# Audio tower on one core: raw loads from a queue of their own, and a new order of calls

## The reference

```python
patches = x[:, :, :n * 16].reshape(B, 90, n, 16) ... -> (B, n, 1440)
h = einsum('bnf,ef->bne', patches, W) + b                        # tokens of 192
h = h + causal_attention(layernorm(h), Wq, Wk, Wv)               # one head of 192
y = layernorm(h)
qkv = y @ W_qkv.T + b_qkv + top2_of_8_experts(y, A, B_lora)      # rank 16 each
h = h + softmax(q k^T / 4) v @ W_proj.T + b_proj                 # 12 heads of 16
```

## Time and profile before

| | |
|---|---|
| median of 3 runs | 631.27 us (631.05, 631.27, 634.49) |
| the profiled execution | 629.51 us |
| its span, first to last instruction | 627.8 us |
| PE busy | 577.8 us, 92% |
| DVE, POOL, ACT busy | 497.5, 382.3, 356.1 us (79, 61, 57%) |
| DMA engines, mean share | 61%, 83.15 MB |

### The profile page before, as it was taken

The page is one execution under the profiler, slowest core; times in us unless marked ns, Lnnn a source line. Parts: engine busy times, 40 slices in busy tenths (PEclk is TensorE's granted clock), DMA queues, the critical chain, the costliest instruction groups (busy, mean ns, idle before and its releaser), DMA issues.

```text
span 627.8 us, 20585 instructions
## 1 busy us (share of the span) xinstructions
PE 577.8 (92%) x7811; PEld 520.6 (83%) x7811; DVE 497.5 (79%) x1312; ACT 356.1 (57%) x688; POOL 382.3 (61%) x646
## 2 busy tenths in 40 slices
PE   1879879999999999999999999999999999997784
PEld 1767768888898989998999999898989898776674
DVE  6523665678888888888898989898888889998774
ACT  3637536666666575657666666666665545543431
POOL 7684887987767677677676867677676633221010
PEclk9979889999999999999999999999999999998965
DMA  8795546887675776767677768575867160615511
GB/s 196 175 209 91 132 96 149 147 193 134 166 150 134 147 169 133 171 129 162 137 164 153 165 142 173 131 155 146 157 142 135 34 127 25 131 37 95 103 28 36
DMA packets 60132, 83.15 MB, mean 132 GB/s; under 512 B 11754, under 2 KB 44087, under 8 KB 58499
## 3 DMA queue, kind: packets, MB, share of 16 engines
q1 hardware_dynamic: 60035, 81.85, 61.2%
HBM read 50.24 MB, written 13.57 MB: 102 GB/s over the span
## 4 chain that ended last, share of the span: by engine, by line
PE 79%; DMA 8%; DVE 7%; ACT 2%; issue 2%; SPq 2%; DVEq 0%; ACTq 0%
PE ps_r L1436 24%; PE ps_tok L1428 7%; PE ps_tok L1429 6%; PE ps_tok L1430 6%; PE ps_p L1688 5%; PE ps_s L1675 4%; PE ps_r L1428 4%; PE ps_r L1430 4%; PE ps_r L1429 4%; DMA k<-qk_scratch 3%; PE ps_r L1589 3%; DMA v<-L_tok_W 2%; PE ps_r L1718 2%; PE ps_r L1526 2%; DMA qk_scratch<-qk 1%
## 5 line engine op out<-in xcount | busy, mean ns | idle before, releaser
L730 POOL TENSOR_TENSOR xs<-raw,xs 90x368 f16<-90x368 f32 x188 | 162.5, 888 | 40.7 <-ACT xs L824 40.7
L1428 PE MATMUL ps_tok<-w_tok,xs 128*128 128x192 f16 x576 | 145.3, 252 | 4.0 <-DVE h L1203 1.5
L1429 PE MATMUL ps_tok<-w_tok,xs 128*128 128x192 f16 x576 | 144.3, 250 | 0.0
L1430 PE MATMUL ps_tok<-w_tok,xs 128*128 128x192 f16 x576 | 144.2, 250 | 0.0
L824 ACT ACTIVATE p2T<-ps_p 128x552 f16<-128x552 f32 x64 | 40.2, 628 | 64.0 <-PE ps_p L1688 44.0
L824 ACT ACTIVATE xs<-raw 90x736 f16<-90x736 f32 x96 | 76.4, 805 | 0.0
L1428 PEld LDWEIGHTS ps_tok<-w_tok,xs 128*128 128x128 f16 x576 | 66.2, 115 | 7.5 <-POOL xe L730 2.6
L730 POOL TENSOR_TENSOR xe<-raw,xe 90x368 f16<-90x368 f32 x64 | 55.4, 884 | 23.4 <-ACT xe L824 23.4
L1429 PEld LDWEIGHTS ps_tok<-w_tok,xs 128*128 128x128 f16 x576 | 66.8, 116 | 1.0
L1430 PEld LDWEIGHTS ps_tok<-w_tok,xs 128*128 128x128 f16 x576 | 66.2, 115 | 0.2
L957 ACT ACTIVATE qk<-ps_r,b_qk 128x368 f16<-128x368 f32 x48 | 27.2, 567 | 47.3 <-PE ps_r L1430 47.3
(11 more groups left out here) (178 smaller groups left out, 1594.8 us busy)
## 6 DMA issues: line engine op xcount, KB each, us to landing
raw<-x SPq DMA_DIRECT2D x32, 1035.0 KB, 7.7
qk_scratch<-qk SPq DMA_DIRECT2D x32, 276.0 KB, 2.8
q<-qk_scratch SPq DMA_DIRECT2D x48, 138.0 KB, 4.8
k<-qk_scratch SPq DMA_DIRECT2D x48, 138.0 KB, 5.6
xs<-xe SPq DMA_DIRECT2D x30, 184.0 KB
v<-v2s SPq DMA_DIRECT2D x64, 76.5 KB, 6.4
out<-h2b SPq DMA_DIRECT2D x16, 240.0 KB
xs<-xe SPq DMA_DIRECT2D x15, 149.5 KB
```

The costliest lines, as they stand in the source:

```text
L730: nc.gpsimd.tensor_tensor(lo, src, hi, ALU.subtract).then_inc(s_lo, 1)
L1428: mm(dst, stat[0], mov[0], start=start, stop=False)
L1429: mm(dst, stat[0], mov[1], start=False, stop=False)
L1430: return mm(dst, stat[1], mov[0], start=False, stop=stop)
```

## The change

`load_next` moves from SP's list to ACT's, so the loads of x of groups 2 to 15 are issued by ScalarE, in its own queue. It waits on the same semaphore value as before. The prologue (groups 0 and 1, token weights, early and middle weights) stays on SP as it was. `LAG`, `MOVED`, `RING_AT`, `STEPS` and the order of the calls in all five lists are new, and `MOVED` now has an entry for the first five and the last five groups instead of three. No arithmetic, tile or buffer changes; PE makes the same 758 calls.

```diff
@@ step_of
-    if op in MOVED and g < 3:
+    if op in MOVED and g < ENDS:
         return at - MOVED[op][n][g]
-    if op in MOVED and g >= GROUPS - 3:
-        return at + MOVED[op][n][g - GROUPS + 6]
+    if op in MOVED and g >= GROUPS - ENDS:
+        return at + MOVED[op][n][g - GROUPS + 2 * ENDS]
+ENDS = 5
-STEPS = 35
+STEPS = 37
@@ SP's step
-                def load_next(half):
-                    g = group(s, "load_next", half)
-                    if g is not None and g > 1:
-                        sp.wait_ge(s_lo, lows_done(g - 1, (8, 16)[half]))
-                        load_x(clips(g, half), half)
@@ ACT's step
+                def load_next(half):
+                    g = group(s, "load_next", half)
+                    if g is not None and g > 1:
+                        act.wait_ge(s_lo, lows_done(g - 1, (8, 16)[half]))
+                        nc.scalar.dma_start(raw[:, half, :, :], clips(g, half)).then_inc(s_x[half], 16)
```

More of the change, by code:

```diff
@@ L54 @@
 LOWS = [(half, blk, part) for half, blk in HIGHS for part in range(2)]
[L57 to L71, removed]
@@ L74 @@
[L74 to L91, removed]
[4 rows of a table removed]
[L96 to L107, removed]
[7 rows of a table removed]
@@ L115 @@
-STEPS = 35
-RING_AT = {"av1": 2, "pv3": 0, "qk1": 2, "cv0": 1, "qk2": 0, "xt0": 2, "cv1": 1, "ot0": 0, "ot1": 2, "pv0": 0,
-           "yt0": 1, "yt1": 0, "pr0": 2, "pr1": 1, "ga": 0, "xt1": 2, "pv1": 0, "g0": 2, "g1": 0, "v0": 1, "v1": 2,
-           "sc": 1, "at": 0, "pv2": 2, "pt": 0, "qk0": 1, "av0": 0}
+LAG = {"place_v2": (13,), "lateload": (6, 8, 9, 9, 10, 10), "extra_rows": (8,), "qk_to_scratch": (12,),
+    "stack_qk": (12,), "store": (14,), "h_to_pairs": (9,), "low": (8, 8, 8, 8, 8, 8, 8, 8, 8, 8, 8, 9, 9, 9, 9, 9),
+    "ad": (12,), "ln1": (9, 10, 10), "h2b": (13,), "ln2": (11,), "xn2": (11,), "xn2_twin": (11,),
+    "wact": (5, 5, 6, 6, 7, 9), "ga_copy": (12,), "g_high": (11, 11), "router_exp": (12,), "load_next": (7, 8),
+    "v_copy": (11, 11), "exp2": (13, 13, 13, 14), "p2t_high": (13, 13, 14, 14), "high": (8, 8, 8, 8, 8, 8, 8, 8),
+    "xn_tile": (10, 10, 10), "ad_high": (12,), "exp1": (11,), "p1t": (11,), "xn_twin": (10,), "o2_twin": (14,),
+    "cv_high": (12, 12), "qk_high": (12, 12, 12), "xn_high": (10, 10), "o_high": (14, 14), "x2_high": (11, 11),
+    "fin": (13, 13), "shift": (11, 11, 11, 12), "logits": (10,), "ranks": (10,), "g_low": (9, 9), "dispatch": (10,),
+    "wdve": (3, 5, 6, 6, 6, 7), "h_tile": (7, 7, 8), "norm2": (11, 12, 12, 12), "p2t_low": (11, 11, 12, 12),
+    "max1": (9,), "stats1": (7, 7, 8), "ad_low": (10,), "max2": (11, 11, 11, 11), "h2": (9, 9), "stats2": (9,),
+    "cv_low": (10, 10), "qk_low": (10, 10, 10), "xn_low": (8, 8), "o_low": (12, 12), "x2_low": (9, 9), "ga": (11,),
[3 rows of a table added]
@@ L123 @@
+STEPS = 37
+RING_AT = {"ga": 0, "pr1": 2, "g0": 0, "g1": 1, "v0": 2, "pv1": 0, "v1": 1, "sc": 2, "at": 0, "pv2": 1, "pt": 2,
+           "pv3": 1, "av0": 0, "av1": 2, "cv0": 1, "qk0": 0, "qk1": 2, "cv1": 1, "qk2": 0, "xt0": 2, "ot0": 1,
+           "pv0": 0, "ot1": 2, "yt0": 1, "yt1": 0, "xt1": 2, "pr0": 1}
 HIGH_AFTER = (0, 0, 0, 0, 9)
@@ L503, in unit_bank, with clips @@
             return (ps_s, ps_p)[n // 2 % 2][0:rows, n % 2, 0:cols]
+        def clips(g, half):
+            b0 = g * GB + half * (GB // 2)
+            return x_v[:, b0:b0 + GB // 2, 0:NT * PATCH]
         block = ctx.enter_context(nc.Block())
@@ L645, in store @@
                             sp.dma_start(out_v[rows, g * PAIRS:(g + 1) * PAIRS, :], h2b[rows, g % 2, :, :]).then_inc(s_out[g % 2], 16)
-                late_weights(5)
[L648 to L652, removed]
-                stack_qk()
-                late_weights(1)
-                late_weights(2)
-                late_weights(4)
-                store()
-                extra_rows()
-                load_next(0)
-                late_weights(0)
+                place_v2()
+                late_weights(1)
+                extra_rows()
+                late_weights(4)
+                qk_to_scratch()
+                late_weights(2)
+                late_weights(0)
+                stack_qk()
+                store()
+                h_to_pairs()
+                late_weights(3)
+                late_weights(5)
             for s in range(STEPS):
@@ L790, in h2b_ @@
                                                 ALU.add).then_inc(s_h2b, 1)
+                low(11)
+                low(12)
                 low(13)
                 low(14)
-                ln1(2)
                 low(15)
+                ad_()
+                ln1(1)
                 low(0)
                 low(1)
-                ln2()
-                xn2_()
-                xn2_twin()
+                ln1(2)
+                h2b_()
                 low(2)
@@ L808, in step @@
                 low(9)
+                ln2()
+                xn2_()
+                xn2_twin()
+                low(10)
                 ln1(0)
-                ln1(1)
-                ad_()
-                low(10)
-                low(11)
-                h2b_()
-                low(12)
             for s in range(STEPS):
@@ L1026, in step @@
                 weights(0)
-                p2t(2)
-                router_exp()
-                g_high(0)
-                high(5)
-                g_high(1)
-                v_copy(0)
-                high(6)
-                weights(3)
-                exp2(3)
+                weights(2)
+                ga_copy()
+                g_high(0)
+                g_high(1)
+                router_exp()
+                load_next(1)
+                v_copy(0)
+                exp2(3)
+                p2t(2)
                 v_copy(1)
-                high(7)
+                high(0)
+                weights(5)
+                xn_tile(0)
                 ad_high()
+                exp1()
                 p2t(3)
-                weights(1)
-                exp1()
-                exp2(0)
+                high(1)
+                high(2)
                 p1t()
-                xn_tile(0)
-                qk_high(0)
                 xn_tile(1)
                 xn_tile(2)
-                high(0)
-                high(1)
+                weights(1)
+                high(3)
+                xn_twin()
+                exp2(0)
+                high(4)
+                weights(3)
+                o2_twin()
+                high(5)
+                cv_high(0)
+                qk_high(0)
                 qk_high(1)
                 p2t(0)
-                cv_high(0)
-                exp2(1)
+                cv_high(1)
                 qk_high(2)
                 xn_high(0)
-                o2_twin()
-                cv_high(1)
-                weights(5)
+                exp2(1)
+                o_high(0)
+                high(6)
                 weights(4)
-                o_high(0)
-                weights(2)
                 o_high(1)
-                xn_twin()
-                high(2)
                 p2t(1)
+                load_next(0)
                 x2_high(0)
+                exp2(2)
                 x2_high(1)
-                exp2(2)
-                high(3)
-                high(4)
-                ga_copy()
                 xn_high(1)
+                high(7)
             for s in range(STEPS):
@@ L1363, in fin @@
                                                        op0=ALU.mult, op1=ALU.add).then_inc(s_fin, 1)
+                fin(0)
+                shift(3)
+                logits()
+                fin(1)
+                ranks()
+                g_low(0)
+                g_low(1)
+                dispatch()
+                weights(2)
+                h_tile(2)
+                norm2(1)
+                p2t(2)
+                weights(0)
+                max1()
+                stats1(2)
                 ad_low()
@@ L1731, in pr @@
                         last.then_inc(p_pr, 1)
[L1734 to L1766 removed]
+                ga_()
+                tok(9)
+                pr(1)
                 tok(10)
                 g_(0)
+                g_(1)
+                p_(2)
+                v_(0)
                 tok(11)
[L1770 to L1772 removed]
+                weights(5)
+                pv(1)
                 v_(1)
[L1774 removed]
                 sc()
+                tok(0)
                 at()
@@ L1778, in step @@
                 p_(3)
-                weights(4)
-                s_(1)
-                tok(0)
-                tok(1)
-                weights(0)
-                pt()
-                qk_(0)
-                av(0)
+                tok(1)
+                s_(0)
+                pt()
+                tok(2)
+                weights(0)
+                tok(3)
+                weights(2)
+                pv(3)
+                av(0)
+                s_(1)
+                av(1)
+                weights(3)
+                cv(0)
+                qk_(0)
+                weights(1)
+                qk_(1)
+                p_(0)
```

(19 more changed lines are left out.)

124 lines of the change are left out of this document (51 added, 73 removed), and 41 rows, old and new, of tables (LAG, MOVED).

## The result

| | before | after |
|---|---|---|
| median of four | 632.9 us | 664.7 us |
| the profiled execution | 629.51 us | 662.83 us |
| its span | 627.8 us | 661.1 us |
| PE busy in the span | 577.8 us | 585.4 us |

The kernel before was run a fourth time beside the changed one (634.52 us), so its median here is 632.9 and not the 631.27 of the three runs that the forecast started from. The changed kernel takes 1.049 times as long, with an interval of 1.040 to 1.057: it is slower by some 32 us. The forecast was 631.2 and the range ended at 637.

A forecast was written before the change was run, and what follows sets the result against it. PE was taken to bound the middle, all 33.25 us of a step, so only the ramps could move: 629.5 + 0.7 (up) - 0.8 (down) = 629.4 us profiled, 631.2 as median; range 622.5 to 637, the forecast's own 628 to 634.4.

The forecast's parts named there:

- The loads ... so 0: Loads of x: they come earlier, but even the old times would do before tok0/2, so 0 us.
- would leave the sum as it is: DMA queues: the new queue brings no bandwidth and loads now share with q and k transfers; no change to the sum.
- 0 is taken: Load issues on ScalarE: 2 x 0.53 us in a step, hidden where ACT is idle for 12 us, so 0.
- Item 1: Ramp up, wpe0: fewer token calls ahead, so PE's wait for Wv grows from 1.9 to 5.6 us, +3.7.
- Item 2: Ramp up, behind wpe0: nine token calls fill PE's 1.6 us wait for DVE before wpe1, -1.6.
- Item 3: Ramp up, 46 to 85 us: token calls between producer and consumer remove small PE waits, -2.6, bounds -3.3 and 0.
- Item 4: Ramp up, yt0/0: ln2/0 on POOL stands behind ten low calls instead of two, +2.8, bounds 0 and +5.
- Item 5: Ramp up, ga/0: weights(5) no longer ahead of x2_low/0 on DVE, so the 3.7 us wait falls to about 1, -2.7.
- Item 6: Ramp up, qk0/0: the same 6.7 us on DVE now stand ahead of h2_/1, +2.3, bounds 0 and +3.5.
- Item 7: Ramp up, clock: four low-clock stretches behind holes become three, at 1.2 us each, -1.2, bounds -3 and +1.5.
- Rival (c): Middle, yt0, xt1 and pr0: DVE frees them late, 0.3 to 0.5 us in 12 steps, 635 to 637 us, chance 0.15.
- The ramp down: From 518 us to the end: same shape, -1.3 at at/15, +2.5 behind it, -2.0 behind s0/15; sum -0.8, bounds -4 and +3.

The follow-up runs named there:

- e1_new_sp: The changed kernel with its new order, but the loads of x back in SP's list: 644.6 us, 1.019 times before.
- e7_wpe0: New order with loads on SP, but PE's first weights put back between tok10/0 and g_/tok11/0: 644.07 us, 1.025 times before.
- e6_w5: The kernel before with only weights(5) of DVE moved behind ad_low of group 0: 631.66 us against 631.35, 1.005.
- e5_tail: New order with loads on SP, and on PE from step 24 on s_(1) ahead of pv(3): 647.3 us, 1.031 times before.
- e4_act_later: The kernel before, old order, with loads of x on ScalarE and half 0's load behind high(6) of the next step: 633.4 us, 1.007 times before.
- e9_new_later: The changed kernel with load_next(0) moved behind high(7) on ScalarE: 658.1 us, 1.041 times before.

## Why the prediction was wrong

The step that failed is "The loads ... so 0", and beside it the sentence that the Trainium skill's rule "would leave the sum as it is". It cost 20 of the 33 us that the runs above part (664.7 - 631.5). The rule (DMA: Bandwidth & Descriptors, section Issuing engines are not separate DMA queues) says that such DMAs interleave on the same 16 engines; the traces agree, with the 22.2 us from the scratch write to `s0/0` instead of 12.5. I had even written that the loads "used to stand in line with the q and k transfers" and now share with them, and then gave that no price. It had one that could be bounded: a load takes 7.7 us, q and k 4.8 and 5.6, so a transfer that meets a load may land up to a load's time later, and the first s0 had no slack at all (it waited 0.27 us before). The bound of one meeting, an estimate from these rows, is 7 to 8 us; the trace showed 9.7 for the round trip, which met two. The other term of that paragraph, "0 is taken" for the issues on ScalarE, was right.

The second failed step is the order, forecast as -0.1 together and measured as +13.1. In the profiled executions e1_new_sp is 642.5 - 627.8 = 14.7 us longer: 5.8 us of it up to the last token call (forecast +0.7), 8.9 behind it (forecast -0.8).

- **Item 1** (+3.7 at `wpe0`) came as said: a wait of 6.53 us in the changed kernel, 5.05 in e1_new_sp, for 1.89. **Item 2** too: the wait of 1.57 us is gone.
- **Item 3** (-2.6) failed in sign. From 46 to 85 us PE is idle for 3.3 us before and for 39.0 - 31.75 = 7.25 us in e1_new_sp, of which 1.4 are item 4's wait ahead of `yt0/0`: +2.5. (The changed kernel is idle for 7.15 us there, 2.9 of them its wait for the extra rows.) I took the waits that I saw as gone and did not ask which new ones the new neighbours bring: 1.31 us for `gT` and 1.18 for `h` at a token call are two of them.
- **Item 4**: the wait ahead of `yt0/0` is 1.47 us, forecast 2.8. **Item 5**: 0.49 us are left ahead of `ga/0`, where I had left 1. **Item 6**: 2.77 us ahead of `qk0/0`, forecast 2.3. The reading of these chains was good to about 1.3 us.
- But adding such items was not sound. e7_wpe0 and e6_w5 show it: take 2.3 or 3.7 us out of one place, and the last token call ends where it ended (522.8 us for 523.2) or 1.3 us later (518.7 for 517.4). In e7_wpe0 the time went straight into the wait for the extra rows of group 1. I take it that the ramp goes by when the first q and k come back and when each group's x parts are ready, and that a hole ahead of these is given back; no run shows this beyond the two.
- **Item 7** (-1.2): the clock of the first 141 us is 0.94 before, 0.95 in e1_new_sp and 0.92 in the changed kernel. For the order alone the sign was right; the waits of the second queue turned it round.
- **The middle**: the steps themselves are as forecast; e1_new_sp loses 0.25 us in it. Rival (c) did not come.
- **The ramp down**, forecast -0.8: from the last token call to the end e1_new_sp takes 119.3 us, before 110.4, so +8.9, though the new order has 1 us less of work left there. Busy times of the two parts, cut at the start of `ga/15` (columns as in the earlier trace rows). Before, then e1_new_sp:

```profile
517.40:567.70 50.30, 46.90 (x693) 39.98 (x692) 47.10 (x125) 26.80 (x56) 14.30 (x26) 1.00 0.33 70
567.70:627.80 60.10, 42.20 (x610) 36.73 (x607) 41.24 (x91) 18.84 (x36) 4.50 (x3) 0.78 0.31 61
```

```profile
523.20:579.30 56.10, 50.13 (x694) 42.37 (x691) 47.64 (x123) 27.20 (x55) 15.30 (x30) 0.92 0.34 75
579.30:642.50 63.20, 42.67 (x612) 37.24 (x610) 40.58 (x89) 19.27 (x36) 4.49 (x3) 0.82 0.28 54
```

  The larger loss, 5.8 us, lies ahead of `ga/15`, in a stretch that I never read: I had compared the lists only from `ga/15` on. There PE is idle 2.6 us more, and busy 3.2 us more for no more work, which fits the low clock behind the wait at 529.46. (In e7_wpe0, with the same lists there and the same wait, the clock is at 0.50 for half as long, from 531.2 to 534.6 us.) The lists give a reason for that wait. Without token calls, `s0` and `pt` alone stand between `p_(3)` and `pv(3)` in the new order (0.8 us of PE); in the old one `s1`, `pt`, `qk0`, `av0`, `av1` and `p0` do, some 4 us. The token calls had been the cover. This is argued from lists and rows; e5_tail tried only one repair, which failed.
- Behind `ga/15` three items missed. At `at/15` I took off 1.3 us for `s0/14`, and a wait of 2.36 us for DVE's `o` stands there in e1_new_sp (2.67 in the changed kernel). The way through HBM is 611.8 - 598.0 = 13.8 us and not 12.2, since the write to scratch lands 1.6 us later; why is open. The chain behind `s0/15` is 30.7 us, before 31.4: -0.7, forecast -2.0. `at/15` to `qk2/15`, forecast 11.0 us, took 11.4.

In short: most single waits were read well, the shared resource was named and not priced, holes were added up in a ramp that gives them back, and the lists of the ramp down were compared over half of it only.

## What to carry to other kernels

Before a large transfer gets a queue of its own, list the urgent transfers that stood ahead of it in the old queue: the old order was their priority. Price one meeting of the two at the large one's own landing time, wherever the urgent one has no slack. If the move is wanted all the same, place the issue some microseconds behind the urgent one, as e4_act_later did for 19 us; whether there is room for that depends on the order (e9_new_later found room for 6.6 of 20 us). In ramps, ask which calls lose their cover when the filling calls run out, and don't add up holes: find the chain that is last at the end of the ramp.
